# Moving the edge encoder beside the first plain pass, numbering edge groups from the last, and unrolling the gathers of the edge convolution

## The reference, cut to what matters

```python
def _L0_gnn_ref(...):                       # label propagation
    for _ in range(3):
        out = clip(0.9 * segment_sum(norm[:, None] * out[row], col) + res, 0, 1)
def _L1_gnn_ref(...):                       # edge-conditioned convolution with a GRU
    eh = relu(e_feat @ en1_w.T + en1_b)     # 200000 x 128
    w_e = (eh @ en2_w.T + en2_b).reshape(-1, 32, 32)
    for _ in range(6):
        msg = einsum('ei,eio->eo', out[src], w_e)
        m = relu(segment_sum(msg, dst) + conv_bias)
        h = gru_cell(m, h, ...); out = h
def _L2_gnn_ref(...):                       # one plain graph convolution
def _L3_gnn_ref(...):                       # one plain convolution with self loops
```

## Time and profile before

| What | us |
|---|---|
| Median of 3 runs | 29634.66 (29593.76 to 29645.51) |
| Profiled execution, its own time | 29624.24 |
| Its span | 29622.5 |
| POOL busy | 18912.0 (64% of the span) |
| PE busy | 15680.3 (53%) |
| DVE busy | 8084.4 (27%) |
| ACT busy | 5957.2 (20%) |

### The profile page before, as it was taken

How to read it: one execution, slowest core, us unless ns; L and a number is a source line. 1 busy time by engine, 2 the same in 40 slices (tenths; PEclk the granted TensorE clock), 3 DMA queues, 4 the chain that set the end, 5 groups by cost and what they waited for, 6 DMA issues and landing times. The chain is left out here.

```text
span 29622.5 us, 431499 instructions
## 1 busy us (share of the span) xinstructions
PE 15680.3 (53%) x96083; PEld 12493.8 (42%) x96083; DVE 8084.4 (27%) x16291; ACT 5957.2 (20%) x14071; POOL 18912.0 (64%) x20031
## 2 busy tenths in 40 slices
PE   3333841221221258867876886886787788112112
PEld 3333421121121246655655664665565567112112
DVE  5444521111111123323332332332333233101111
ACT  0000510000000023423433442342343344000000
POOL 4887047757757657737737746774773774675775
PEclk5555965555555578988887897897888789555555
DMA  3222622322322324534433443452443444222222
GB/s 99 49 49 49 219 79 46 51 40 47 51 39 47 49 75 113 128 77 107 125 89 100 121 117 78 114 128 74 110 126 86 103 122 106 40 48 46 42 48 43
DMA packets 5514647, 2428.17 MB, mean 82 GB/s; under 512 B 4822474, under 2 KB 5290186, under 8 KB 5392764
## 3 DMA queue, kind: packets, MB, share of 16 engines
q1 hardware_dynamic: 4404056, 1640.66, 22.4%
q0 software_dynamic: 650176, 469.34, 9.1%
q10 hardware_dynamic: 459168, 307.23, 3.3%
HBM read 1850.82 MB, written 557.33 MB: 81 GB/s over the span
## 5 line engine op out<-in xcount | busy, mean ns | idle before, releaser
L763 POOL DMA_INDIRECT sb_xg<-node_rows,sb_idx x9408 | 8927.8, 949 | 3157.0 <-issue 2669.3
L982 POOL DMA_INDIRECT sb_xg<-node_rows,sb_idx x7840 | 7408.0, 945 | 3516.3 <-issue 2387.0
L870 PE MATMUL banks<-sb_spread,sb_eh_sb 128*128 128x256 f32 x29184 | 8029.2, 437 | 2228.8 <-DMA sb_eh_sb<-eh 2226.1
L870 PEld LDWEIGHTS banks<-sb_spread,sb_eh_sb 128*128 128x128 f32 x29184 | 6288.2, 221 | 3674.0 <-issue 2113.2
L826 DVE TENSOR_TENSOR sb_spread<-sb_xs,banks_p 128x2048 f32<-128x2048 f32 x1824 | 4172.0, 2288 | 9161.5 <-PE banks L870 8892.0
L924 ACT ACTIVATE sb_g<-banks 128x512 f32<-128x512 f32 x7296 | 4357.2, 597 | 7152.2 <-PE banks L870 7027.5
L1074 PE MATMUL banks_s<-sb_mask,sb_xs 128*128 128x32 f32 x6080 | 1452.1, 403 | 7744.8 <-DMA sb_xs<-gathered_rows 7744.8
L1074 PEld LDWEIGHTS banks_s<-sb_mask,sb_xs 128*128 128x128 f32 x6080 | 1353.5, 328 | 7844.7 <-issue 7301.3
L1050 DVE COPY sb_s<-banks_s 32x32 f32<-32x32 f32 x3040 | 568.3, 187 | 8437.2 <-PE banks_s L1074 8292.2
L343 POOL DMA_INDIRECT slots<-sb_rows,sb_slot_u x1600 | 2106.2, 1316 | 774.5 <-issue 757.7
L1145 ACT ACTIVATE sb_stat<-sb_stat 98x64 f32<-98x64 f32 x4 | 1.0, 256 | 10853.0 <-DVEq L1137 10853.0
(11 more groups left out here) (212 smaller groups left out, 9388.4 us busy)
## 6 DMA issues: line engine op xcount, KB each, us to landing
sb_eh_sb<-eh SPq DMA_DIRECT2D x912, 1024.0 KB
sb_xs<-gathered_rows SPq DMA_DIRECT2D x26752, 16.0 KB
sb_xg<-node_rows,sb_idx POOLq DMA_INDIRECT x17248
eh<-sb_eh_sb ACTq DMA_DIRECT2D x304, 512.0 KB, 3.2
gathered_rows<-sb_xg POOLq DMA_DIRECT2D x588, 256.0 KB
gathered_rows<-sb_xg ACTq DMA_DIRECT2D x980, 128.0 KB, 1.7
sb_win_row<-window_rows SPq DMA_DIRECT2D x100, 488.3 KB
slots<-sb_zeros SPq DMA_DIRECT2D x19, 2368.0 KB
```

What stands on the lines that cost most here:

```text
L763: nc.gpsimd.indirect_dma_start(m.xg_two[h][:, t * D:(t + 1) * D], None, m.node_dram, bass.IndirectOffsetOnAxis(ap=m.idx_two[h][:, t:t + 1] ...
L870: o = mm(m.ps_pair[u % 4][:, v, :, :], m.eh[h % 2][:, t * K:(t + 1) * K], m.spread[t // TS][:, t % TS, :, :], start=True, stop=True)
L982: nc.gpsimd.indirect_dma_start(m.xg[h][:, t * D:(t + 1) * D], None, m.node_dram, bass.IndirectOffsetOnAxis(ap=m.idx[h][:, t:t + 1], axis=0 ...
```

## The change

Three things change.

1. `encode_edges` becomes `unpack_rows`, with 152 steps of 16 tiles. It keeps sources, metadata, masks and degrees, and no longer turns, encodes or stores anything of the attributes. The encoding moves into the first plain pass (`encode=True`), where each batch also has: on SP one load of the records (264 KB) and one store of 1 MB of `eh`; on DVE one unpacking copy of 128x512, one copy of 128x512 out of PSUM and one maximum with zero of 128x2048 out of PSUM; on PE four transposes and eight matmuls of 128x512, of which four add the bias from a row of ones. `rectify` of batch n also waits until the `eh` of batch n-2, which used the same buffer, is stored. The other two propagation steps stay in a loop with `encode=False`.
2. The window key is 783 minus the window. The 86 empty tiles come first (`PAD`), then the sparse windows, and the full windows are last.
3. In the convolution, POOL's loop is written out: 1568 gathers whose index is a column of `src_c`, without the copy of indices. Blocks have 32 rows (47 of them, then 16, 16, 16, 8, 8); the block before is stored after the third gather of a block and counted after its seventh. `landed` now counts 8 rows at a time.

```diff
-JC, JBODIES = 8, 49
+JC, JBODIES, JL = 8, 49, 32
+PAD = TP - (EDGES - 1) // P - NW
@@ prepare_edges
+            do(V.tensor_scalar(m.win[:, :], m.tmp_i[:, :], -1.0, float(NW - 1), ALU.mult, ALU.add))
+            do(V.tensor_copy(m.key_i[:, :], m.win[:, :]))
+            do(V.tensor_scalar_add(m.win[:, :], m.win[:, :], float(PAD)))
@@ place_windows
+            do(V.tensor_scalar_add(m.first[:, :], m.first[:, :], float(PAD)))
-            do(V.tensor_scalar(m.row_of[:, :], m.row_of[:, :], 1.0, float(JT - 1), ALU.add, ALU.min))
+            do(V.tensor_scalar(m.row_of[:, :], m.row_of[:, :], float(1 - PAD), 0.0, ALU.add, ALU.max))
@@ unpack_rows: vector, then tensor
+                    V.tensor_copy(m.meta_t[:, bass.ds(n * TC * 3, TC * 3)].rearrange("s (t r) -> s t r", r=3),
+                                  rows[:, :, 1:4]).then_inc(meta_kept, 1)
...
+                    for t in range(TC):
+                        s = nc.tensor.matmul(m.ps_deg[h % 2][:, t * WN:(t + 1) * WN], rows[:, t, 2:META],
+                                             m.mask[h][:, t, :], start=True, stop=True)
@@ conv_pass
+    sizes = [JL] * 47 + [16, 16, 16, 8, 8]
+            for b in range(len(sizes)):
+                for t in range(sizes[b]):
+                    row = starts[b] + t
+                    nc.gpsimd.indirect_dma_start(
+                        m.xg_two[b % 2][:, t * D:(t + 1) * D], None, m.node_dram,
+                        bass.IndirectOffsetOnAxis(ap=m.src_c[:, row:row + 1], axis=0)).then_inc(got[b % 2], 16)
+                    if b > 0 and t == 2:
+                        keep(b - 1)
+                    if b > 0 and t == 6:
+                        count(b - 1)
-                    sp.wait_ge(landed, ((rows[TS - 1] >> 4) & 127) + 1)
+                    sp.wait_ge(landed, ((rows[TS - 1] >> 3) & 255) + 1)
@@ plain_pass(nc, m, weight, after, encode=False), sync
+            def fetch_attr(i, n, h):
+                sp.wait_ge(unpacked, n + 1)
+                sp.dma_start(m.row_buf[h % 2], slots_v[:, bass.ds(n * TC * ROW, TC * ROW)]).then_inc(attr_in[h % 2], 16)
+            def store_eh(i, n, h):
+                sp.wait_ge(relu, n + 2)
+                sp.dma_start(m.eh_dram[:, bass.ds(n * TC * K, TC * K)], m.eh[h % 2]).then_inc(eh_out[h % 2], 16)
+                skewed(sp, (fetch_attr, 0), (fetch, 0), (store, 4), (store_eh, 4))
@@ vector
+            def unpack(i, n, h):
+                dve.wait_ge(attr_in[h % 2], i * 32 + h // 2 * 16 + 16)
+                dve.wait_ge(turned, n + 1)
+                V.tensor_copy(m.attr[h % 2].rearrange("s (t f) -> s t f", f=D),
+                              m.row_buf[h % 2].rearrange("s (t r) -> s t r", r=ROW)[:, :, META:ROW]).then_inc(unpacked, 1)
+            def copy_turned_rows(i, n, h):
+                dve.wait_ge(turned, n + 3)
+                dve.wait_ge(encoded, n + 1)
+                V.tensor_copy(m.attr_t[h % 2], m.ps_turn).then_inc(turned_sb, 1)
+            def rectify(i, n, h):
+                dve.wait_ge(encoded, n + 3)
...
+                V.tensor_scalar_max(m.eh[h % 2].rearrange("s (g x) -> s g x", g=4), m.ps_eh, 0.0).then_inc(relu, 1)
+                skewed(dve, (masks, 0), (copy_sums, 2), (copy_out, 2), (unpack, 0), (copy_turned_rows, 1), (rectify, 2))
@@ tensor
+            def encode_rows(i, n, h):
+                pe.wait_ge(turned_sb, n + 2)
+                pe.wait_ge(relu, n + 1)
+                for g in range(4):
+                    mm(m.ps_eh[:, g, :], m.ones[:, :], m.en1_b[0:1, :], start=True, stop=False)
+                    me = mm(m.ps_eh[:, g, :], m.attr_t[h % 2][:, g * P:(g + 1) * P], m.en1[:, :], start=False, stop=True)
+                skewed(pe, (turn_rows, 0), (encode_rows, 1), (sum_and_project, 0))
@@ propagate
+    step(True)
+    with nc.Fori(1, STEPS0):
+        step(False)
```

More of the change, by code:

```diff
@@ L545, in encode @@
-            def encode(i, n, h):
-                for g in range(2):
-                    pe.wait_ge(turned_sb, n * 2 + g + 3)
-                    pe.wait_ge(biased, n * 2 + g + 1)
-                    nc.tensor.matmul(m.ps_eh[g], m.attr_t[2 * (h % 2) + g], m.en1[:, :], start=True,
-                                     stop=True).then_inc(eh_ps, 1)
-            staged(pe, turn_and_sum, encode, 1)
+            with pe.Fori(0, BODIES) as i:
+                for h in range(L):
+                    n = i * L + h
+                    rows = m.rowin[h].rearrange("s (t r) -> s t r", r=ROW)
+                    pe.wait_ge(rows_in[h], i * 16 + 16)
+                    pe.wait_ge(masked, n + 1)
+                    pe.wait_ge(deg_sb, n + 1)
+                    for t in range(TC):
+                        s = nc.tensor.matmul(m.ps_deg[h % 2][:, t * WN:(t + 1) * WN], rows[:, t, 2:META],
+                                             m.mask[h][:, t, :], start=True, stop=True)
+                    s.then_inc(degs, 1)
@@ L584, in _ @@
-            staged(act, copies, rectify, 2)
+            act.sem_inc(deg_sb, 2)
+            for i in peeled(act, BODIES):
+                for h in range(L):
+                    n = i * L + h
+                    act.wait_ge(degs, n + 1 + L)
+                    wait_after_first(act, deg_out[h], i * 16)
+                    nc.scalar.activation(m.deg_s[h], m.ps_deg[h % 2], ACT.Copy).then_inc(deg_sb, 1)
+                    act.wait_ge(deg_sb, n + 3)
+                    act.dma_start(m.deg_dram[:, bass.ds(n * TC * WN, TC * WN)], m.deg_s[h]).then_inc(deg_out[h], 16)
@@ L771, in _, with keep, count @@
-            keep(JBODIES - 1, 2 * JBODIES - 1, 1)
-            for h in range(2):
-                pool.wait_ge(put[h], JBODIES * 16)
-                pool.sem_inc(landed, 1)
+            def keep(b):
+                pool.wait_ge(got[b % 2], lane(sizes, b))
+                row = starts[b]
+                pool.dma_start(m.xg_dram[:, row * D:(row + sizes[b]) * D], m.xg_two[b % 2][:, 0:sizes[b] * D]).then_inc(
+                    put[b % 2], 16)
+            def count(b):
+                pool.wait_ge(put[b % 2], b // 2 * 16 + 16)
+                pool.sem_inc(landed, sizes[b] // 8)
@@ L776, in _ @@
+            keep(len(sizes) - 1)
+            count(len(sizes) - 1)
         @block.sync
@@ L945, in _, with plain_pass @@
                 act.wait_ge(stored[h], BODIES * 16)
-def plain_pass(nc, m, weight, after):
+def plain_pass(nc, m, weight, after, encode=False):
     GT, GJ = 16 * TC, 16 * JC
@@ L1020, in store @@
                 sp.dma_start(m.part_dram[bass.ds(n * TC * WN, TC * WN), :], m.part[h]).then_inc(stored[h], 16)
-            skewed(sp, (fetch, 0), (store, 4))
+            def fetch_attr(i, n, h):
+                sp.wait_ge(unpacked, n + 1)
+                hold(sp, held_sp)
+                sp.dma_start(m.row_buf[h % 2], slots_v[:, bass.ds(n * TC * ROW, TC * ROW)]).then_inc(attr_in[h % 2], 16)
+            def store_eh(i, n, h):
+                sp.wait_ge(relu, n + 2)
+                hold(sp, held_sp)
+                sp.dma_start(m.eh_dram[:, bass.ds(n * TC * K, TC * K)], m.eh[h % 2]).then_inc(eh_out[h % 2], 16)
+            if encode:
+                skewed(sp, (fetch_attr, 0), (fetch, 0), (store, 4), (store_eh, 4))
+                for h in range(2):
+                    sp.wait_ge(eh_out[h], BODIES * 32)
+            else:
+                skewed(sp, (fetch, 0), (store, 4))
             for h in range(L):
@@ L1083, in add_tiles @@
+            if encode:
+                pe.sem_inc(turned, 2)
+                pe.sem_inc(encoded, 2)
+                skewed(pe, (turn_rows, 0), (encode_rows, 1), (sum_and_project, 0))
+            else:
+                skewed(pe, (sum_and_project, 0))
 def add_tiles(nc, m):
@@ L1220, in _, with step @@
                 store_nodes(sp, m, m.y, ready, stored)
-    scaled_state(m.x)
-    with nc.Fori(0, STEPS0):
-        plain_pass(nc, m, 1, m.fold)
+    def step(encode):
+        plain_pass(nc, m, 1, m.fold, encode)
         add_tiles(nc, m)
@@ L1538, in build @@
         m.eh = [eh[:, h] for h in range(2)]
-        m.eh_e = [eh[:, h // 2, (h % 2) * EC * K:(h % 2 + 1) * EC * K] for h in range(L)]
-        m.en1, m.en1_b = sb("en1", [P, 4 * K]), sb("en1_b", [P, 4 * K])
+        m.en1, m.en1_b, m.ones = sb("en1", [P, 4 * K]), sb("en1_b", [P, 4 * K]), sb("ones", [1, P])
         m.x, m.h, m.y = (sb(n, [NQ, NM * D]) for n in ("x_sb", "h_sb", "y_sb"))
@@ L1587, in _ @@
                     do(nc.vector.memset(x, 0.0))
+                do(nc.vector.memset(m.ones[:, :], 1.0))
         propagate(nc, m)
```

209 lines of the change are left out of this document (73 added, 136 removed).

## The result

The changed kernel takes 28,263.6 us (median of 4 runs, 28,262.3 to 28,266.4) against 29,634.3 us (4 runs beside it, 29,593.8 to 29,645.5): a ratio of 0.954, with a 95% interval of 0.9523 to 0.9556. It is faster, but the gain is 1371 us where 2535 were forecast, and 28,264 lies above the upper end of the range, 28,050.

The account below looks back on a forecast made before the run. It took POOL's gathers to bound the plain passes, gathers then PE the convolution. Terms -663-15-336-1524+3 (extra vector work) = -2535 us from 29,624.24 gave 27,089, on the median 27,100 us; range 26,850 to 28,050.

Parts of the forecast that it names:

- What bounds the kernel: Whole kernel before: plain passes bound by POOL's gathers (1960 us); convolution passes by gathers first, then PE and its feed.
- Part 1: Encoding stage of 943 us: becomes an unpacking stage of 152 steps at 1.7 us, 280 us in all, -663 us.
- the 6.8 us cycle: Unpacking stage: load landing 3.8, DVE 0.7, PE 1.1, waits 1.2 us; over four buffers 1.7 us a step.
- The lower bound of 190: Unpacking stage: shortest time in us, from 41 MB at 217 GB/s.
- Part 2: First plain pass with the encoder in it: 13.1 us a batch, 2050 us against 2065, -15 us.
- Rival B: First plain pass: pauses keep PE at 1.2 GHz, 19.4 us a batch, +959 us, total 28,060; chance 0.10.
- SP's 12.6 us a batch: First plain pass, SP's queue: 11.1 us a batch before, plus two more DMAs with waits at 0.75 us each.
- The 87 us: First plain pass: 152 new copies at 0.57 us, each shutting POOL out for its length; total 27,190; forecast took nothing.
- Part 3: Four other plain passes: gathers stay at 1960 us, each tail falls from 105 to 21 us, -336 us.
- Part 4: Six convolution passes: each falls from 2294 to 2040 us, PE's pace of 12.87 us a batch setting it, -1524 us.
- The sign that I had named: Convolution passes, trace of after: 2040 us each, with L870 at 12.9 us a batch from first to last.
- The range: Whole kernel: 26,850 to 28,050 us, from D's end (everything hides, 26,900) to B's and C's (28,060, 28,020); about 0.15 outside.

## Why the prediction was wrong

**What bounds the kernel** held for the kernel before: gathers at 1.25 us set its plain passes, and gathers at first and consumers at the end its convolution passes. What was worked out from it for the changed kernel's convolution did not hold; see part 4.

**Part 1** (-663) came out at -743 for the stage, -739 up to the first gather. The stage takes 200 us: its DMA engines are 80% busy at 231 GB/s, and VectorE waits for a load in each of the 152 steps, 120 us in all. A step takes 1.32 us and not 1.7: the terms of the 6.8 us cycle were too large (a load lands in 3.2 us where I took 3.8). The lower bound of 190 was worked out from a wrong size: a load is 296 KB and not 264, the whole 46 MB and not 41, which at 217 GB/s would be 212 us. The stage beat that because it moved 231.

**Part 2** (-15, in truth +1219) is the step that failed, and in it one sentence: "PE is busy 75% here, so I add 1 us". I took the granted clock as a function of TensorE's busy share, from two rows with matmuls of 128 rows each, and carried it over to a stream of which half reads one row. An earlier sentence, that a bias from a row of ones costs as much as the matmul itself, was true of time and hid what it does to the clock. The runs put in its place: 0.50 with 1, 32 and 64 rows, 0.82 with 128, 0.70 with the one-row matmuls bundled, 0.71 without them. Of the 1234 us against the forecast, the row count explains 968. The 198 of the register loads show only once the clock is up. The last 68 are open: even then a batch takes 13.8 us where I had 13.1. Rival B named the right state and the right total (28,060, 200 low), but for the wrong reason, the pauses; its shortfall is about the alternation, 2.4 us a batch, which no row of before showed. It got a chance of 0.10.
SP's 12.6 us a batch was also low. Its stream is 15.1. Of the 2.5 us between, 1.4 are the two register loads, taken at their length in a pass without large transfers beside it; with short ones it is still 13.8. The new copy of 512 columns took 0.44 us (mean of 89, 3300 to 5200 us) and not 0.57. That is 0.15 for 256 columns more, where copies out of PSUM have 0.27 (0.69 for 512, 2.29 for 2048), so my reading that a copy within SBUF has the plain rate was wrong. Taking nothing for it was nearly right all the same: gathers filled 1964.7 us beside it and 1960.0 before. The 87 us that the rule of the Trainium skill (SBUF — State Buffer, "Who interferes with whom") would have added didn't appear with this copy. With the bias on VectorE something like them did: its maximum over 2048 columns goes from SBUF to SBUF (1.26 us), the 151 gathers that it overlapped from 3400 to 5200 us took 1.47 us each in place of 0.95, and the gathers of the pass filled 2058 us, 93 more, hidden there by SP's stream. There the trace agrees with the rule.

**Part 3** (-336) measured -325: tails of 21.5 against the forecast 21, and gathers some 3 us longer a pass.

**Part 4** (-1524) measured -1515, the right number by another path. I had let TensorE's pace of 12.87 us a batch set the whole pass, with the gathers under it all along: 76+152*12.87 = 2032, and 7 us for the last `eh`. In the changed kernel the consumers take 11.5 us a batch, by which their line would end at 76+152*11.5 = 1824; they catch up with the gathers near batch 100, and the pass is then the gathers' 2001 us and a tail of 40. That 2041 meets the forecast 2040 is luck. The sign that I had named, L870 (now L804) at 12.9 a batch from the first to the last, is missed: 11.5 at first, 17 at the end. The gathers took 2001 us and not 1991; the stalls in the written-out stream, which I had put at nothing, are some 12 of it (POOL waits for landings 3.6 us in the 600 from 13300).

**The sum.** -739+1219-325-1515 = -1360, which is the difference of the spans. Parts 1, 3 and 4 together were forecast at -2523 and came to -2579. With the clock and SP's stream mended the kernel takes 27,063, near the forecast 27,100, but in part by luck: in its profiled execution (27,106) part 1 is 80 us better than forecast, part 2 68 worse, and parts 3 and 4 together 31 worse. **The range** failed with its upper end set at a rival's point value: B had terms of its own (a matmul at twice 0.86 us) and no margin for them.

## What to carry to other kernels

A busy TensorE isn't enough to raise its clock. When a small matmul (a bias from a row of ones, a short contraction) joins a stream, look at the rows it uses and at the granted clock beside the busy share. Spread it over all rows, bundle such matmuls, or give the sum to another engine. In a queue written out by hand, put register loads behind small issues, not behind the biggest transfer. When a rival gives a bound of the range, give it a margin of its own. And when a total comes out right, look at the pace along the stage before you believe the path: the convolution pass met its forecast within a microsecond and was bound by another engine.

## What the runs showed of the hardware

- TensorE stayed at 1.2 GHz through the whole first plain pass, 3283 us at 89% busy, when half of its long matmuls read one of 128 rows; with 32 or 64 rows the pass was as long and the clock 0.50 too. With 128 rows it was granted 0.82 at 69% busy.
- At that clock a record of a 512-column fp32 matmul takes 0.85 us in a run of its kind and 1.00 us where one-row and 128-row matmuls alternate.
- A register load of SP took 0.55 us on average, and 1.24 with up to 2.96 where one of two stood behind a 1.3 MB burst on its own queue.
- A copy of 512 fp32 columns by VectorE took 0.44 us within SBUF and 0.69 out of PSUM. Gathers that overlapped a 1.26 us maximum from SBUF to SBUF took 1.47 us in place of 0.95.
- The same convolution code ran at 11.5 us a batch with the encoder in the plain pass and at 12.9 with the encoder in a stage of its own.
- One chip ran the three kernels tried there 1.6 to 1.7 times as long. In a plain pass, gathers took 1.39 us in place of 1.25. While they ran, SP needed 0.68 us for each small register instruction (0.04 on the other chips) and 0.72 for each issue (0.34); once they had ended both were as elsewhere, and batches went on for 1500 us. What ailed the chip stays open.
